# The remainders of the state's half 1 move from VectorE to GpSimd, and one of the 24 products of a step moves behind the close of half 0

## The reference, cut to what matters

```python
# x: (4, 512, 256), cond: (4, 256)
x = x + L0(x, cond)        # adaptive low-rank block, ends in a residual of its own
xW = einsum('ntd,dh->nth', x, Wx) + b
def step(prev_h, xw_t):
    next_h = tanh(xw_t + prev_h @ Wh)
    return next_h, next_h
_, hs = lax.scan(step, h0, swapaxes(xW, 0, 1))     # h0 = cond, T = 512 steps
return x + swapaxes(hs, 0, 1)
```

## Time and profile before

| | us |
|---|---|
| median of 3 runs | 555.61 |
| lowest, highest | 550.74, 555.97 |
| profiled execution, its own time | 551.53 |
| its span, first to last instruction | 549.7 |
| between span and time | 1.8 |
| PE busy | 511.1 (93%) |
| VectorE busy | 296.5 (54%) |
| ScalarE busy | 176.5 (32%) |
| GpSimd busy | 21.9 (4%), all before 39 us |

### The profile page before, as it was taken

The page is one execution under the profiler, slowest core; times in us unless marked ns, Lnnn a source line. Parts: engine busy times, 40 slices in busy tenths (PEclk is TensorE's granted clock), DMA queues, the critical chain, the costliest instruction groups (busy, mean ns, idle before and its releaser), DMA issues.

```text
span 549.7 us, 32433 instructions
## 1 busy us (share of the span) xinstructions
PE 511.1 (93%) x14388; PEld 439.2 (80%) x14388; DVE 296.5 (54%) x2262; ACT 176.5 (32%) x1154; POOL 21.9 (4%) x34
## 2 busy tenths in 40 slices
PE   6988999999999999999998999899999989998995
PEld 4224777899999999999998888888888888888884
DVE  1154666555656555565555555555555555555553
ACT  2010222333333434333333333333333333333322
POOL 2850000000000000000000000000000000000000
PEclk7698999999999999999999999999999999999998
DMA  8950000000000000000000000000000000000000
GB/s 295 383 185 2 3 4 3 13 5 14 4 13 5 14 4 4 16 4 14 4 14 5 14 4 14 4 7 11 5 14 4 13 5 13 4 14 5 8 9 12
DMA packets 11346, 16.01 MB, mean 29 GB/s; under 512 B 1715, under 2 KB 7106, under 8 KB 11202
## 3 DMA queue, kind: packets, MB, share of 16 engines
q1 hardware_dynamic: 10352, 13.37, 7.4%
q10 hardware_dynamic: 854, 0.57, 0.4%
HBM read 11.85 MB, written 2.10 MB: 25 GB/s over the span
## 4 chain that ended last, share of the span: by engine, by line
PE 89%; ACT 5%; issue 2%; DVE 1%; DMA 1%; ACTq 0%; DVEq 0%
PE bank L833 65%; PE bank L762 7%; ACT w_sb L429 5%; PE bank L803 3%; PE bank L808 3%; PE bank L656 2%; PE bank L790 2%; PE bank L649 1%; DMA beta_sb<-in_L_cond_ln_beta 1%; PE bank L771 1%; PE bank L635 1%; PE bank L757 1%; PE bank L671 1%; PE bank L820 1%; PE bank L676 0%
## 5 line engine op out<-in xcount | busy, mean ns | idle before, releaser
L833 PE MATMUL bank<-w_sb,whp 128*128 128x52 bf16 x6132 | 243.0, 186 | 25.1 <-ACT w_sb L429 24.8
L591 DVE TENSOR_TENSOR r_ring<-w_sb 128x4 f32<-128x4 f32 x1022 | 136.5, 163 | 211.6 <-ACT w_sb L429 207.7
L429 ACT ACTIVATE w_sb<-bank 128x4 f32<-128x4 f32 x1024 | 142.0, 173 | 320.8 <-PE bank L833 320.8
L833 PEld LDWEIGHTS bank<-w_sb,whp 128*128 128x128 bf16 x6132 | 188.7, 96 | 68.4 <-ACT w_sb L429 46.4
L833 PE MATMUL bank<-r_ring,whp 128*128 128x52 bf16 x4096 | 219.9, 185 | 0.1
L833 PEld LDWEIGHTS bank<-r_ring,whp 128*128 128x128 bf16 x4096 | 173.9, 96 | 0.2 <-issue 0.2
L833 PE MATMUL bank<-l_ring,whp 128*128 128x52 bf16 (+1 forms) x2048 | 156.4, 177 | 0.0
L596 DVE TENSOR_TENSOR l_ring<-r_ring 128x4 bf16<-128x4 f32 x1024 | 136.3, 162 | 0.0
L833 PEld LDWEIGHTS bank<-l_ring,whp 128*128 128x128 bf16 x2048 | 121.6, 96 | 0.0
L762 PE MATMUL bank<-xp,wxp 128*128 128x32 bf16 x1536 | 71.6, 177 | 0.0
L762 PEld LDWEIGHTS bank<-xp,wxp 128*128 128x128 bf16 x1536 | 54.0, 96 | 0.0
(11 more groups left out here) (109 smaller groups left out, 192.3 us busy)
## 6 DMA issues: line engine op xcount, KB each, us to landing
w_sb<-in_L_cond_W SPq DMA_DIRECT2D x16, 512.0 KB, 10.8
x_sb<-in_x SPq DMA_DIRECT2D x4, 512.0 KB, 11.2
out<-o_sb SPq DMA_DIRECT2D x64, 32.0 KB, 1.6
down_sb<-in_L_cond_base_down SPq DMA_DIRECT2D x1, 256.0 KB, 5.2
w_sb<-in_L_cond_W ACTq DMA_DIRECT2D x1, 256.0 KB, 5.6
up_sb<-in_L_cond_base_up ACTq DMA_DIRECT2D x1, 256.0 KB, 9.0
wx_sb<-in_L_cond_Wx SPq DMA_DIRECT2D x1, 256.0 KB, 10.2
wh_sb<-in_L_cond_Wh SPq DMA_DIRECT2D x1, 256.0 KB, 10.4
```

The costliest lines, as they stand in the source:

```text
L429: nc.scalar.activation(h_ring[:, m, slot(pair, s), 0:B], zt, ACT.Tanh).then_inc(h_ready, 1)
L591: nc.vector.tensor_tensor(r_ring[:, k, q, 0:B], state_before(pair, s, k)[:, 0:B], state_hi_before(pair, s, k)[:, 0:B], ALU.subtract).then_ ...
L833: return nc.tensor.matmul(zbank(p, q, m)[:, col0:col0 + n], whp[part][:, k, P * m:P * (m + 1)], rhs[:, 0:n], start=False, stop=stop, skip_ ...
```

## The change

The semaphores `r_ready` and `l_ready` become two each, one per half. The two instructions a step for half 1 (r and l) leave VectorE's queue and become the only work of GpSimd in the recurrence: `residues` there waits for `h_ready` of half 1, computes r, waits for its own `r_ready[1]`, computes l. VectorE keeps r and l of half 0. On PE the product of part 1 of Wh with r of half 0 into output half 1 moves from the fourth place behind the 12 to the place right behind the close of output half 0: 19 products up to that close, five behind it. The number of products stays 24, and of small instructions 4 a step.

```diff
@@ gpsimd
             nc.gpsimd.memset(h_ring[:, :, :, B:W], 0.0).then_inc(pad_ready, 1)
+            def residues(pair, first, last):
+                for s in range(PAIR):
+                    q, step = s % 2, PAIR * pair + s
+                    pool.wait_ge(h_ready, 2 * step + 2)
+                    nc.gpsimd.tensor_tensor(r_ring[:, 1, q, 0:B], state_before(pair, s, 1)[:, 0:B],
+                                            state_hi_before(pair, s, 1)[:, 0:B], ALU.subtract).then_inc(r_ready[1], 1)
+                    pool.wait_ge(r_ready[1], step + 1)
+                    nc.gpsimd.tensor_tensor(l_ring[:, 1, q, 0:B], r_ring[:, 1, q, 0:B], r_hi[:, 1, q, 0:B],
+                                            ALU.subtract).then_inc(l_ready[1], 1)
+            over_pairs(residues)
@@ vector, residues
-                    for k in range(K2):
-                        dve.wait_ge(h_ready, 2 * PAIR * pair + 2 * s + k + 1)
-                        ... r of half k ...
-                    for k in range(K2):
-                        dve.wait_ge(r_ready, 2 * PAIR * pair + 2 * s + k + 1)
-                        ... l of half k ...
+                    step = PAIR * pair + s
+                    dve.wait_ge(h_ready, 2 * step + 1)
+                    ... r of half 0 ... .then_inc(r_ready[0], 1)
+                    dve.wait_ge(r_ready[0], step + 1)
+                    ... l of half 0 ... .then_inc(l_ready[0], 1)
@@ tensor, recurrence
-                    pe.wait_ge(r_ready, done + 1)
-                    for m in range(K2):
-                        for part in range(2):
-                            product(part, 0, m, r_hi[:, 0, q, :])
-                    pe.wait_ge(r_ready, done + 2)
+                    pe.wait_ge(r_ready[0], step + 1)
+                    for part in range(2):
+                        product(part, 0, 0, r_hi[:, 0, q, :])
+                    product(0, 0, 1, r_hi[:, 0, q, :])
+                    pe.wait_ge(r_ready[1], step + 1)
                     for part in range(2):
                         product(part, 1, 0, r_hi[:, 1, q, :])
-                    pe.wait_ge(l_ready, done + 1)
+                    pe.wait_ge(l_ready[0], step + 1)
                     product(0, 0, 0, l_ring[:, 0, q, :])
-                    pe.wait_ge(l_ready, done + 2)
+                    pe.wait_ge(l_ready[1], step + 1)
                     product(0, 1, 0, l_ring[:, 1, q, :], stop=True).then_inc(z_ready, 1)
+                    product(1, 0, 1, r_hi[:, 0, q, :])
                     for part in range(2):
                         product(part, 1, 1, r_hi[:, 1, q, :])
                     product(0, 0, 1, l_ring[:, 0, q, :])
                     product(0, 1, 1, l_ring[:, 1, q, :], stop=True).then_inc(z_ready, 1)
```

More of the change, by code:

```diff
@@ L197, in adaptive_lowrank_then_recurrence @@
         h_ready = sem("h_ready")
-        r_ready = sem("r_ready")
-        l_ready = sem("l_ready")
+        r_ready = [sem(f"r_ready{k}") for k in range(K2)]
+        l_ready = [sem(f"l_ready{k}") for k in range(K2)]
         z_ready = sem("z_ready")
@@ L588, in residues @@
                     tile, i = 2 * pair + s // TS, s % TS
-                    for k in range(K2):
-                        dve.wait_ge(h_ready, 2 * PAIR * pair + 2 * s + k + 1)
-                        nc.vector.tensor_tensor(r_ring[:, k, q, 0:B], state_before(pair, s, k)[:, 0:B],
-                                                state_hi_before(pair, s, k)[:, 0:B],
-                                                ALU.subtract).then_inc(r_ready, 1)
-                    for k in range(K2):
-                        dve.wait_ge(r_ready, 2 * PAIR * pair + 2 * s + k + 1)
-                        nc.vector.tensor_tensor(l_ring[:, k, q, 0:B], r_ring[:, k, q, 0:B], r_hi[:, k, q, 0:B],
-                                                ALU.subtract).then_inc(l_ready, 1)
+                    step = PAIR * pair + s
+                    dve.wait_ge(h_ready, 2 * step + 1)
+                    nc.vector.tensor_tensor(r_ring[:, 0, q, 0:B], state_before(pair, s, 0)[:, 0:B],
+                                            state_hi_before(pair, s, 0)[:, 0:B], ALU.subtract).then_inc(r_ready[0], 1)
+                    dve.wait_ge(r_ready[0], step + 1)
+                    nc.vector.tensor_tensor(l_ring[:, 0, q, 0:B], r_ring[:, 0, q, 0:B], r_hi[:, 0, q, 0:B],
+                                            ALU.subtract).then_inc(l_ready[0], 1)
                     if not (last and s >= TS):
@@ L828, in recurrence @@
                     col0 = B * (s % TS // 2)
-                    done = 2 * PAIR * pair + 2 * s
+                    step = PAIR * pair + s
+                    done = 2 * step
                     def product(part, k, m, rhs, stop=False):
```

## The result

The changed kernel takes 642.47 us (median of four runs, 641.7 to 643.63) against 553.2 us for the kernel before (four runs, 550.74 to 555.97; three of them are those of the table before). The ratio is 1.161, 95% interval 1.157 to 1.166: slower by 16%. The profiled execution took 641.72 us, span 639.9.

What follows compares the result with a forecast made beforehand. Two latency loops of 0.94 us a step, through half 0 and half 1, were taken to bind; the new half 1 loop sums to 1.077, so 490 x 0.135 = 66 us on 551.5 gives 618 us, range 592 to 676.

Steps and rivals of the forecast that it cites:

- the forecast side: Main case: no blocking, full clock, GpSimd wake-up plus duration between 0.21 and 0.29; 580 to 655 us, likeliest 618, chance 57%.
- wake-up of GpSimd, two times: GpSimd starting r after tanh, and l after r: 0.08 us each, between 0.04 and 0.12 after tanh.
- GpSimd's r and l: Half 1's two subtractions on GpSimd: 0.172 us each, from a line through 256- and 512-element rows.
- close to close, with the fifth product: PE between the closes of half 0 and half 1: one more product lengthens 0.11 to 0.14 us.
- The upper bound of 0.225: Longest duration allowed per GpSimd subtraction, from another 256-element row; would give a period of 1.183 and 669 us.
- closing product's wait for l: PE in the kernel before: waiting for l of half 1 costs no more than 0.01 us, so both loops bind.
- The covered steps: About 20 steps bounded by PE's large fills: l of half 1 arrives in time there, cost zero, leaving 490 periods.
- VectorE's relief: VectorE's queue losing two instructions a step, 0.104 us each: nobody waited for that queue, so zero gain.
- The rival of blocking: VectorE and GpSimd subtractions hold each other up, l of half 1 0.09 us later: 662 us, chance 20%.
- The clock rival: PE's granted clock falls in parts, period 1.26 against 1.077; 18 us if 100 steps are struck, 636 us; 15%.
- The rival on the other side: Half 1's remainders come early enough, so the loop of half 0 binds at 0.915: faster, 538 us, chance 3%.
- w: GpSimd's wake-up and duration together for one subtraction: put at 0.25 us; below 0.184 half 1's loop beats 0.94.

Runs made afterwards that it cites:

- Experiments six and seven: Changed kernel with GpSimd's two subtractions taking 12 columns (six) or 52 columns (seven) instead of 4, the added ones zeros: 652.26 us and 719.23 us.
- experiment three: Changed kernel with GpSimd's two subtractions replaced by memsets of the same 128 x 4 numbers, waits and order kept: 535.59 us, ratio 0.967 to the kernel before.
- experiment two: Changed kernel with PE's product moved back, 20 products up to the close and four behind; half 1's remainders stay on GpSimd: 630.87 us, ratio 1.140.
- experiment eight: Changed kernel with GpSimd's r of half 1 replaced by a memset of 128 x 200 numbers that reads nothing: 672.15 us.
- experiment five: Changed kernel with halves swapped, GpSimd computing half 0's remainders and VectorE half 1's, 20 products up to the close, four behind: 596.02 us, ratio 1.079.

## Why the prediction was right, and what was mis-sized

The measured 642.47 lies in the range, on the forecast side, 24 us above the 618. The mechanism, a longer loop through half 1 with everything else covered, is the one that the trace shows. Term by term (us; the measured ones are typical of the steps between 100 and 500 us):

| term of the new loop | predicted | measured |
|---|---|---|
| tanh | 0.173 | 0.173 |
| wake-up of GpSimd, two times | 0.08 | 0.077 and 0.079 |
| GpSimd's r and l | 0.172 each | 0.198 and 0.200 |
| end of l to the closing product 19 | 0.06 | 0.057 |
| close to close, with the fifth product | 0.14 | 0.140 |
| second close to tanh 1 | 0.20 | 0.204 |
| sum | 1.077 | 1.128 |

The failed term is the duration. "The line through both has 1.93 ns an element and 0.164 us at none; four elements give 0.172 us": the two rows were 256 and 512 elements long, one of them on 3 partitions, and I carried their line down to four. It was 0.027 short, two times a step: 490 x 0.054 = 26 us, and 618 + 26 = 644. The upper bound of 0.225 took it in. Experiments six and seven show the bend; what makes it is not shown.

The wake-up of 0.08, which no row showed from ScalarE to GpSimd, was right: I had taken it from GpSimd's waits on itself because VectorE's two kinds were equal. That the two kinds are equal on GpSimd as well was a guess that held.

The closing product's wait for l in the kernel before, which I put at no more than 0.01 us, was 0.003 and cost the loop of half 0 0.013 with what followed (experiment three). The forecast did not hang on it, since that loop stopped binding.

The covered steps held. Between 54 and 96 us there are now 34 to 35 pairs of tanh, and again 21 of 511 periods are far over the rest; in these the fills of PE hide GpSimd's chain, as the earlier trace rows let expect. VectorE's relief was worth nothing: its wait for tanh grew, and the fills behind its l had slack before.

The rival of blocking was real and cost some 1 us. VectorE's l of half 0 is held for 0.024 us, ends at 478.68, and PE wants it at 478.76. The step in my price that failed is the second one: I let VectorE's held l run to full length behind GpSimd's r and hold GpSimd's l in turn. Held, it ends 0.012 after GpSimd's r, and GpSimd's l starts 0.08 after the end of that r, so nothing of it is left to hold the l. What did hold GpSimd's l, in 63 steps, was almost always a larger VectorE instruction that began 0.136 before it: it then took 0.214 us, and the step was 0.015 longer, 1 us in all against the 0.28 a step that I had feared. Even held for 0.1 us, with 52 columns, VectorE's l added nothing: the period there, 1.276 most often, is 1.128 + 2 x 0.074, the two longer instructions alone. And experiment two, where VectorE's l lasts 0.162, is faster by the fifth product's 0.025 only.

The clock rival did not come at 1.128 us a step, where the granted clock is 1.00, that is 2.4 GHz, from 54 us to the last 2 us of the span (the PEclk line of the page above shows it slice by slice). In experiment eight, at 1.177, the granted clock was 0.98 between 300 and 400 us and 0.96 between 400 and 500. It fell more often at 1.276. With 52 columns, stretches of 200 us from 100 and 300 on (length, busy PE, PEld, DVE, ACT, POOL, granted clock, DMA):

```profile
100.00:300.00 200.00, 184.57 (x4458) 157.27 (x4457) 83.74 (x377) 60.20 (x363) 85.13 (x313) 1.00 0.03 6
300.00:500.00 200.00, 179.21 (x4283) 149.94 (x4279) 75.29 (x357) 55.51 (x343) 84.80 (x312) 0.92 0.02 6
```

In the second, where the fills have become fewer, the clock is at 1.2 GHz in parts (PE was busy 92% of the first stretch and 90% of this one). GpSimd still does 312 instructions in it, two a step, against 313: the slower products found room in PE's wait for GpSimd. A step that lies wholly at 1.2 GHz is 1.36 us there, 0.083 longer than the others, and 1.26 in experiment eight, again 0.083; I had 1.26 against 1.077 for the changed kernel, 0.18 a step. My 18 us for this rival would have been too much. In the profiled execution of experiment two, at 1.103 us a step, the granted clock read 0.95 in every 100 us from 96 us on; it took 632.81 us, the other three 630.65 to 631.06. Why is not shown.

The rival on the other side, at w below 0.184 for wake-up and duration, has its measured end in experiment three: 535.6 us, where I had 538. GpSimd's w is 0.277, and the subtraction would have to lose a third of it to break even.

## What to carry to other kernels

Where two loops of one step are in balance, moving an instruction to another queue helps only if the queue was the wait: look whether the instruction started at its queue's pace or at its input's. Price a small instruction on another engine by wake-up plus duration at its own size, and do not carry a line through large instructions down to four elements; here an idle GpSimd was 0.08 us dearer for each of two dependent subtractions. And moving a product from before one close to behind it is free only for the loop that does not pass the second close.

## What the runs showed of the hardware that was not expected

- A GpSimd subtraction of 128 x 4 takes 0.198 us and one of 128 x 12 takes 0.205, against 0.163 for VectorE's of 128 x 4; a GpSimd memset of 128 x 4 takes 0.102.
- A VectorE subtraction with two SBUF operands that takes 0.163 us by itself ends 0.01 to 0.02 us after a GpSimd subtraction that started 0.02 us before it (0.187, 0.200, 0.267 us behind one of 0.198, 0.205, 0.272); beside a memset of 0.265 us it keeps its 0.162. A GpSimd subtraction that is held ends 0.06 to 0.07 us after VectorE's instruction (0.214 us instead of 0.198 in the changed kernel, 0.205 in experiment five, 0.324 to 0.328 in experiment eight). So the hold costs what is left of the first instruction, and not that plus the whole second one.
- The first product behind a wait on PE is followed by the next after 0.038 or 0.039 us, not 0.025 (the 12 products behind a tanh, and the closing product behind l), and from a closing product to the next tanh it is 0.215 us where that product had to wait and 0.204 where not.
